# Retention results kept heads by tokens, per-token numbers spread through DRAM, and a new order of work

## What is computed

```
scores = einsum('bhtd,bhsd->bhts', q, k) * mask
denom  = clip(abs(scores).sum(-1, keepdims=True), 1.0, 50000.0)
ret    = einsum('bhts,bhsv->bthv', scores / denom, v)
ret    = ret * rsqrt(mean(ret * ret, axis=-1, keepdims=True) + EPS)
out    = ((x @ W_g + b_g) * ret) @ W_o + b_o
xn     = x / max(norm(x), 1e-12) * sqrt(C) * gamma          # soft mixture
logits = xn @ slots; dispatch = softmax over tokens; combine = softmax over slots
```

## Time and profile before

| | us |
|---|---|
| median of 3 runs (1097.90 to 1098.71) | 1098.13 |
| the profiled execution | 1098.24 |
| its span | 1096.4 |
| PE busy | 1062.8 |
| DVE busy | 960.2 |
| ACT busy | 773.0 |
| POOL busy | 606.9 |

### The profile page before, as it was taken

How to read it: one execution, slowest core, us unless ns; L and a number is a source line. 1 busy time by engine, 2 the same in 40 slices (tenths; PEclk the granted TensorE clock), 3 DMA queues, 4 the chain that set the end, 5 groups by cost and what they waited for, 6 DMA issues and landing times.

```text
span 1096.4 us, 27975 instructions
## 1 busy us (share of the span) xinstructions
PE 1062.8 (97%) x10436; PEld 832.9 (76%) x10436; DVE 960.2 (88%) x2074; ACT 773.0 (71%) x1450; POOL 606.9 (55%) x619
## 2 busy tenths in 40 slices
PE   5799999999999999999999999999999999999997
PEld 3478687787868778687787868778687787868776
DVE  3788989899898988989899898988989899898985
ACT  3476786767777676786767777676786767777674
POOL 2465547556474665547556474655647556474553
PEclk9899999999999999999999999999999999999998
DMA  6000000000000000000000000000000000000000
GB/s 257 11 2 11 1 20 3 1 21 1 21 1 11 11 1 22 1 12 10 2 21 1 21 1 2 20 2 21 2 11 11 2 20 2 21 1 2 11 1 20
DMA packets 18468, 16.97 MB, mean 15 GB/s; under 512 B 800, under 2 KB 17440, under 8 KB 18080
## 3 DMA queue, kind: packets, MB, share of 16 engines
q1 hardware_dynamic: 18336, 15.18, 4.2%
HBM read 10.98 MB, written 4.19 MB: 14 GB/s over the span
## 4 chain that ended last, share of the span: by engine, by line
PE 90%; DVE 6%; issue 1%; ACT 1%; POOL 0%; POOLq 0%; DVEq 0%; ACTq 0%
PE bank L1008 12%; PE bank L959 11%; PE bank L969 10%; PE bank_s L990 7%; PE bank L950 5%; PE bank L979 5%; PE bank L920 5%; PE bank L913 5%; PE bank L1035 3%; DVE ret L661 3%; PE bank L908 3%; PE bank L823 3%; PE bank L874 3%; PE bank L1018 3%; PE bank_s L993 2%; PE bank L854 2%
## 5 line engine op out<-in xcount | busy, mean ns | idle before, releaser
L329 POOL TENSOR_TENSOR ret_abs<-ret_abs 128x512 f32<-128x512 f32 x128 | 168.7, 1318 | 238.2 <-ACT ret_abs L485 238.2
L661 DVE TENSOR_TENSOR ret<-bank_s,k_sb 128x1536 f32<-128x1536 f32 x128 | 223.9, 1749 | 23.7 <-PE bank L1008 14.8
L334 POOL TENSOR_TENSOR urs<-uvar,mhalf 128x16 f32<-128x16 f32 x64 | 185.3, 2903 | 91.8 <-DVE uvar L677 91.8
L485 ACT ACTIVATE ret_abs<-ret 128x1536 f32<-128x1536 f32 x128 | 189.6, 1481 | 8.8 <-DVE ret L661 8.8
L959 PE MATMUL bank<-slotsT,w_sb 128*128 128x128 f32 x1024 | 140.9, 281 | 0.3 <-DVE hact L726 0.3
L969 PEld LDWEIGHTS bank<-w_sb,hact 128*128 128x128 f32 x1024 | 125.5, 192 | 14.7 <-issue 13.9
L969 PE MATMUL bank<-w_sb,hact 128*128 128x128 f32 x1024 | 134.1, 277 | 0.0
L959 PEld LDWEIGHTS bank<-slotsT,w_sb 128*128 128x128 f32 x1024 | 124.3, 192 | 10.3 <-issue 7.4
L340 POOL TENSOR_SCALAR dT<-dT,drec 128x256 f32<-128x256 f32 x128 | 83.4, 665 | 48.6 <-DVE drec L721 48.4
L1008 PE MATMUL bank<-ret,vrow 128*32 128x256 f32 (+1 forms) x2048 | 108.6, 329 | 0.3 <-DVE hact L726 0.2
L990 PE MATMUL bank_s<-qT,km 32*128 32x256 f32 x1024 | 91.4, 426 | 5.0 <-DVE ret L661 5.0
(11 more groups left out here) (143 smaller groups left out, 2397.9 us busy)
## 6 DMA issues: line engine op xcount, KB each, us to landing
x_sb<-x SPq DMA_DIRECT2D x16, 256.0 KB, 2.8
w_sb<-w SPq DMA_DIRECT2D x2, 2048.0 KB, 14.8
out<-attn SPq DMA_DIRECT2D x16, 256.0 KB, 2.3
v_sb<-vectors SPq DMA_DIRECT2D x1, 832.0 KB, 8.1
w_sb<-weights SPq DMA_DIRECT2D x1, 512.0 KB, 5.3
k_sb<-consts SPq DMA_DIRECT2D x1, 466.0 KB, 6.6
w_sb<-weights SPq DMA_DIRECT2D x1, 320.0 KB, 3.2
slot_sb<-slot_rows SPq DMA_DIRECT2D x1, 256.0 KB, 3.5
```

Source lines behind the costliest of these rows:

```text
L329: pool.tensor_tensor(both[:, :, P:SEQ], both[:, :, P:SEQ], both[:, :, SEQ:3 * P], ALU.add)\
L334: pool.tensor_tensor(urs[:, j], uvar[:, j], mhalf[:], ALU.pow).then_inc(ready["urs"].sem, 1)
L485: act.activation(ret_abs[:, q % MR], ret[:, q % MR], ACT.Abs).then_inc(ready["ab"].sem, 1)
L661: dve.tensor_tensor(ret[:, q % MR], bank_s[:, :, 0:3 * P], causal.unsqueeze(1).broadcast_to([P, Q, 3 * P]), ALU.mult)\
```

## The change

- `g`: two quads now share a bank. An odd quad's values sit 16 rows lower in each head's 32 rows (the left operand is read 16 columns earlier), and both accumulate, so that a bank holds eight heads by 256 tokens in columns 0 to 255, and in columns 256 to 511 the denominator, repeated over the 16 rows of each head. Instruction count and columns are those of before.
- `RTc`, `row`, `rowd`, `urs`, `gatedT`, `gTc` are gone. Per two quads: `usq` squares (ACT), `ms` multiplies with a block matrix of 1/16 (PE, one call of 256 columns), `den` clips (DVE), `dsq` squares it with scale sqrt(EPS) (ACT), `ug` multiplies with the gate (DVE), `rx` adds mean and EPS * den^2 (DVE). Per pair: `ln` (ACT) and `rs` (ACT, Exp with scale -0.5) over 128x1024 give the root's inverse, and `gated` multiplies 128x512 twice (DVE). `o` reads that directly.
- `vg` makes only values (2 tasks of two 256-column calls); `gT` makes the gates channels by tokens (2 calls of 512 columns), `gTb` adds the bias (ACT).
- `xn3T`, its copy, `rB` and its copy are gone from PE and ACT. SP writes `rnorm` and `rmax` (128x4 each) to a small DRAM tensor, element by element, and reads each back as 512 numbers to all 128 partitions. `xn3Tc` is now a POOL multiplication of xn2T with what came back; `cs` waits for the other.
- The order of every engine and the banks are new; the last six experts, quad 7, the last two `g`, `out` and `o` are now age 2; stores are age 3 in an order for SP.

```diff
-    "PE": [("qk", 0, 1), ("xn3T", 0, 1), ("qk", 1, 1), ("vg", 0, 1), ...
+    "PE": [("h", 2, 2), ("h", 3, 2), ("quad", 7, 2), ("h", 4, 2), ("ms", 2, 2), ("eo", 2, 2), ("h", 5, 2),
+           ("eo", 3, 2), ("h", 6, 2), ("h", 7, 2), ("eo", 4, 2), ("eo", 5, 2), ("g", 6, 2), ("g", 7, 2),
+           ("xn2T", 0, 1), ("eo", 6, 2), ("eo", 7, 2), ("qk", 0, 1), ("ms", 3, 2), ("qk", 1, 1), ("gT", 0, 1),
+           ("vg", 0, 1), ("out", 0, 2), ("quad", 0, 1), ("xnT", 0, 0), ("out", 1, 2), ("LT", 0, 1),
+           ("quad", 1, 1), ("LT", 1, 1), ("LT", 2, 1), ("o", 0, 2), ("LT", 3, 1), ("s", 0, 0), ("quad", 2, 1),
+           ("g", 0, 1), ("g", 1, 1), ("gT", 1, 1), ("e", 0, 0), ("quad", 3, 1), ("global", 0, 0), ("k", 0, 0),
+           ("ms", 0, 1), ("DT", 0, 1), ("vg", 1, 1), ("DT", 1, 1), ("mxT", 0, 1), ("score", 0, 0), ("r", 0, 0),
+           ("quad", 4, 1), ("g", 2, 1), ("g", 3, 1), ("score", 1, 0), ("DT", 2, 1), ("DT", 3, 1), ("quad", 5, 1),
+           ("PT", 0, 0), ("srow", 0, 0), ("slots", 0, 1), ("PT", 1, 0), ("slots", 1, 1), ("ms", 1, 1),
+           ("o", 1, 2), ("v", 0, 0), ("h", 0, 1), ("local", 0, 0), ("h", 1, 1), ("quad", 6, 1), ("g", 4, 1),
+           ("g", 5, 1), ("eo", 0, 1), ("eo", 1, 1)],
+    "DVE": [("ret", 6, 2), ("prod", 0, 1), ("x1", 0, 1), ("eoc", 0, 2), ("ug", 2, 2), ("hb", 2, 2), ("den", 2, 2),
+            ("hb", 3, 2), ("ret", 7, 2), ("stat2", 0, 1), ("hb", 4, 2), ("rx", 2, 2), ("hb", 5, 2), ("xn2", 0, 1),
+            ("eoc", 1, 2), ("hb", 6, 2), ("cs", 2, 2), ("hb", 7, 2), ("stat", 0, 0), ("eoc", 2, 2), ("ug", 3, 2),
+            ("den", 3, 2), ("cs", 3, 2), ("xn3", 0, 1), ("eoc", 3, 2), ("qkc", 0, 1), ("qkc", 1, 1), ("rx", 3, 2),
...
+            ("gbias", 0, 0), ("drec", 1, 1), ("ret", 3, 1), ("rx", 0, 1), ("vgc", 1, 1), ("rmax", 0, 1),
+            ("LTm", 3, 1), ("drec", 2, 1), ("smax", 0, 0), ("drec", 3, 1), ("ret", 4, 1), ("smax", 1, 0),
+            ("cs", 0, 1), ("ug", 1, 1), ("den", 1, 1), ("zg", 0, 2), ("srowc", 0, 0), ("ka", 0, 0), ("ret", 5, 1),
...
+    "ACT": [("sp", 0, 1), ("usq", 2, 2), ("ab", 6, 2), ("hg", 2, 2), ("hg", 3, 2), ("dsq", 2, 2), ("ab", 7, 2),
+            ("hg", 4, 2), ("hg", 5, 2), ("ce", 1, 2), ("hg", 6, 2), ("hg", 7, 2), ("usq", 3, 2), ("xn2Tc", 0, 1),
+            ("ce", 2, 2), ("dsq", 3, 2), ("ce", 3, 2), ("gTb", 0, 1), ("ln", 0, 2), ("rs", 0, 2), ("ab", 0, 1),
...
+    "SP": [("store", 0, 3), ("load", 0, 0), ("fput", 0, 1), ("fget", 0, 1), ("mput", 0, 1), ("rBc", 0, 1)],
...
+            def mput(p, par, k):
+                sp.wait_ge(*ready["rmax"](p))
+                since(sp, max_got, p - 1)
+                sp.dma_start(turn[1].rearrange("(j p) -> p j", p=P), rmax[:], allow_slow_non_contiguous=True).then_inc(max_put.sem, 16)
+
+            def mget(p, par, k):
+                sp.wait_ge(*max_put(p))
+                since(sp, ready["cs"], p - 1, 3)
+                sp.dma_start(rB[:], turn[1].unsqueeze(0).broadcast_to([P, TOK])).then_inc(max_got.sem, 16)
...
+            def xn3Tc(p, par, k):
+                pool.wait_ge(*got(p))
+                pool.wait_ge(*ready["xn2Tc"](p))
+                since(pool, filled["LT"], p - 1, 3)
+                pool.tensor_tensor(xn3T[:], xn2T[:].rearrange("p b n -> p (b n)"), fB[:], ALU.mult).then_inc(ready["xn3Tc"].sem, 1)
...
+            def ln(p, par, k):
+                act.wait_ge(*ready["rx"](p, DUOS - 1))
+                act.activation(rx[:], rx[:], ACT.Ln).then_inc(ready["ln"].sem, 1)
+
+            def rs(p, par, k):
+
+                act.wait_ge(*ready["ln"](p))
+                act.activation(rx[:], rx[:], ACT.Exp, scale=-0.5).then_inc(ready["rs"].sem, 1)
...
+            def rx_(p, par, h):
+                dve.wait_ge(*filled["ms"](p, h))
+                dve.wait_ge(*ready["dsq"](p, h))
+                dve.wait_ge(*ready["ug"](p, h))
+                since(dve, ready["gated"], p - 1, h // 2)
+                dve.tensor_tensor(rx[:, h], banks[BANK["g", 2 * h]][:, SEQ:], den[:, h % 2], ALU.add).then_inc(ready["rx"].sem, 1)
...
+                bank = banks[BANK["g", q - 1]] if i else claim("g", p, q)
...
+                        at = (Q * (q % Q) + n) * HT - i * VD
+                        left = spread[:, 2 * b + sblock, at:at + HT] if phase < 2 else K["count"][:, (1 - i) * VD:(1 - i) * VD + HT]
                         cols = (0, SEQ) if sblock == 0 else (SEQ, 3 * P)
-                        ins = pe.matmul(bank[n * HT:(n + 1) * HT, sblock * P:SEQ], left,
-                                        src[:, q % MR, n, cols[0]:cols[1]], start=(phase == 0), stop=(phase == 2))
+                        into = (phase // 2 * SEQ + sblock * P, (phase // 2 + 1) * SEQ)
+                        ins = pe.matmul(bank[n * HT:(n + 1) * HT, into[0]:into[1]], left, src[:, q % MR, n, cols[0]:cols[1]],
+                                        start=(i == 0 and phase == 0), stop=(i == 1 and phase == 2))
...
+            def ms(p, par, h):
+                pe.wait_ge(*ready["den"](p, h))
+                pe.wait_ge(*ready["ug"](p, h))
+                pe.matmul(banks[BANK["g", 2 * h]][:, SEQ:], K["heads"], usq[:, h % 2], start=True, stop=True)\
+                  .then_inc(filled["ms"].sem, 1)
```

More of the change, by code:

```diff
@@ L50 @@
 ORDER = {
[10 rows of a table removed]
[L61 to L70, removed]
[3 rows of a table removed]
@@ L103 @@
            "score": "P", "PT": "PTc", "local": ("field", 0), "r": ("tr", 0), "k": ("kr", 0), "v": ("rv", 0),
-           "xn2T": ("xn2Tc", 0), "xn3T": ("xn3Tc", 0), "qk": "qkc", "vg": "vgc", "LT": "LTc", "mxT": ("rmax", 0), "rB": ("rBc", 0), "DT": "Dc", "slots": "slc", "h": "hb", "eo": "eoc", "row": "ug", "g": "RTc", "gatedT": "gTc", "o": "attn",
+           "xn2T": ("xn2Tc", 0), "qk": "qkc", "vg": "vgc", "LT": "LTc", "mxT": ("rmax", 0), "DT": "Dc", "slots": "slc", "h": "hb", "eo": "eoc", "g": "rx", "gT": "gTb", "o": "attn",
@@ L172, in build @@
         km = sb("km", KM, SEQ)
-        vrow, grow = sb("vrow", TILES, HEADS, HT), sb("grow", TILES, HEADS, VD)
+        vrow, grow = sb("vrow", TILES, HEADS, HT), sb("grow", 2, TOK)
         ret, ret_abs = sb("ret", MR, Q, 3 * P), sb("ret_abs", MR, Q, 3 * P)
[L175 to L179, removed]
+        usq, den = sb("usq", 2, SEQ), sb("den", 2, SEQ)
+        ug, rx = sb("ug", DUOS, SEQ), sb("rx", DUOS, SEQ)
         attn = sb("attn", TILES, C)
@@ L214, in build @@
             ("prod", 1), ("x1", 1), ("stat2", 1), ("mv2", 1), ("var_eps2", 1), ("rstd2", 1), ("rn", 3), ("rnorm", 1),
-            ("xn2", 1), ("xn3", 1), ("xn2Tc", 1), ("xn3Tc", 1), ("qkc", 2), ("km", QUADS), ("vgc", 4), ("ret", QUADS),
-            ("ab", QUADS), ("add", QUADS), ("RTc", QUADS), ("usq", 4), ("ug", 4), ("den", 4), ("den2", 4), ("ums", 4),
-            ("uvar", 4), ("urs", 4), ("gated", 4), ("gTc", 2), ("attn", 2), ("LTc", 4), ("mx", 3), ("rmax", 1), ("rBc", 1), ("cs", 4), ("ce", 4),
+            ("xn2", 1), ("xn3", 1), ("xn2Tc", 1), ("xn3Tc", 1), ("qkc", 2), ("km", QUADS), ("vgc", 2), ("gTb", 2), ("ret", QUADS),
+            ("ab", QUADS), ("add", QUADS), ("usq", DUOS), ("den", DUOS), ("dsq", DUOS), ("ug", DUOS),
+            ("rx", DUOS), ("ln", 1), ("rs", 1), ("gated", 2), ("attn", 2), ("LTc", 4), ("mx", 3), ("rmax", 1), ("cs", 4), ("ce", 4),
             ("ltmax", 4), ("DTe", 4), ("drec", 4), ("dn", 4), ("Dc", 4), ("slc", 2), ("hb", E), ("hg", E),
@@ L436, in xn2Tc @@
                     .then_inc(ready["xn2Tc"].sem, 1)
-            def xn3Tc(p, par, k):
-                bank = bank_of("xn3T", p)
-                since(act, filled["LT"], p - 1, 3)
-                act.activation(xn3T[:], bank[:], ACT.Copy).then_inc(ready["xn3Tc"].sem, 1)
             def LTc(p, par, m):
@@ L680, in gated_, with den_ @@
-            def gated_(p, par, j):
-                dve.wait_ge(*ready["urs"](p, j))
-                since(dve, filled["gatedT"], *((p, 0) if j >= 2 else (p - 1, 1)))
-                dve.tensor_tensor(gated[:, j % 2].rearrange("p (h v) -> p h v", h=HEADS), ug[:, j],
-                                  urs[:, j].unsqueeze(2).broadcast_to([P, HEADS, VD]), ALU.mult)\
-                   .then_inc(ready["gated"].sem, 1)
+            def den_(p, par, h):
+                dve.wait_ge(*ready["usq"](p, h))
+                since(dve, ready["rx"], *((p, h - 2) if h >= 2 else (p - 1, h + 2)))
+                dve.tensor_scalar(den[:, h % 2], banks[BANK["g", 2 * h]][:, SEQ:], 1.0, 50000.0, ALU.max, ALU.min)\
+                   .then_inc(ready["den"].sem, 1)
@@ new lines, in ug_ @@
+            def ug_(p, par, h):
+                b, u = divmod(h, 2)
+                dve.wait_ge(*ready["usq"](p, h))
+                dve.wait_ge(*ready["gTb"](p, u))
+                since(dve, filled["o"], p - 1, b)
+                dve.tensor_tensor(ug[:, h], banks[BANK["g", 2 * h]][:, 0:SEQ], grow[:, u, b * SEQ:(b + 1) * SEQ], ALU.mult)\
+                   .then_inc(ready["ug"].sem, 1)
+            def rx_(p, par, h):
[4 more added lines that the diff above has]
```

(11 more changed lines are left out.)

226 lines of the change are left out of this document (102 added, 124 removed), and 30 rows, old and new, of tables (BANK, ORDER).

## The result

The change made the kernel slower: 1249.43 us (median of 4, 1248.27 to 1253.09) against 1098.02 for the kernel before, ratio 1.138 (95% interval 1.136 to 1.141). The forecast of 1073 and its range of 1062 to 1093 were wrong; of the rivals, D happened, the slow write of single numbers, to which I had given 0.04.

The account below looks back on a forecast made before the run. PE was taken to bound the kernel: its period of 65.98 us a pair falls to 64.2, other engines hidden. 16 x 64.2 plus ends of 44 is 1071, plus time over the span gives 1073 us; range 1062 to 1093.

Parts of the forecast that it names:

- D: Rival: SP's write by single numbers is slow; at a 12 us trip, 4 us a pair, 1137 us; chance 0.04.
- the price of the write: SP's write of 512 single numbers to DRAM: 2.8 us, bounds 0 and 14.8; 5.6 for a round trip.
- a cover of 4.4: DVE work before cs 0 (LTm, two drec, two smax, ret) that hides rmax's round trip: 4.4 us.
- half of DVE's room: DVE's standing at cs 0 begins to cost at a trip over some 8 us: 5.6 plus half of 5.9.
- about 11 us: covered: PE work before LT 0, about 11 us, hides rnorm's 1.8, the 5.6 round trip and xn3Tc's 1.3.
- PE's step: On PE, 32 transposes removed (3.5 us) and four ms added (1.75): net -1.75 us a pair, period 64.2.
- ACT 51.4 for 50.3: ACT's work a pair, copies removed, new operations and two table loads added: 48.3 becomes 50.3 us, hidden.
- The tables: ACT's table loads: two more a pair, 2.6 us, bounds none and three; six a pair in all.
- The ends: First and last steps, where PE has too little to do: 3 us more (bounds 0 and some 9), 44 us.
- E: Rival: the new order removes small waits and the ends don't grow: 64.0 and 41, 1067 or less; chance 0.09.
- Rival B: PE waits from the four banks, gT 0 for eoc 3: 0.5 to 1.5 us a pair, 1081 to 1097; chance 0.24.
- C: Rival: Rival B's place but worse, DVE late behind PE's claim of bank 2; at 2.6 us, 1115; chance 0.07.

Follow-up runs that it names:

- Experiment 11: e9_mx_strided plus four extra transfers a pair on SP (single-number writes to neighbours, 64 and 512 bytes apart, and a read back): 1069.05 us.
- e9_mx_strided: e5_rows16 with the transposes before rmax taking every fourth token, so cs reads without a stride: 1070.65 us, 0.975 of the kernel before.
- experiment 3: The changed kernel with both numbers spread by PE and ACT again, nothing through DRAM: 1123.6 us, 1.024 of the kernel before.
- e5_rows16: The changed kernel with each DRAM write as 128 pieces of 16 bytes, cs and xn3Tc reading with a stride: 1088.6 us, 0.991 of the kernel before.
- experiments 7, 8 and 10: Against the kernel before: experiment 3 with rB in bank 1, 1.008; e5_rows16 with cs 0 later, 1.007; e9_mx_strided with xn3 and stat2 moved on DVE, 0.996.

## Why the prediction was wrong

**The step that failed** is the price of the write: "The write has as many pieces as that load's rows, but 4 bytes each: nearest row again 2.8". It took 8.7 us. The count of pieces was taken for what sets a write's time. Experiment 11 shows that it is where they go: 8.9 us against 1.6 to 2.6 with the same count. The read back is a second miss of that step, 4.8 to 4.9 us to landing by the page where the load of x takes 3.0. A trip was 13.7 us, not 5.6. My bound reached to 14.8 for the write alone, so the value was inside it, but it didn't reach the chances: D got 0.04. With 14.8 for the write a trip is 17.6, by D's own price 9.6 us a pair and 1227 us; with a cover of 4.4 the change's sign hung on that term, and the range should have said so.

**D's arithmetic held for half.** It said 4 us a pair at a trip of 12, and from there a microsecond for each microsecond of trip; at 13.7 that is 5.7. Measured against e9_mx_strided, which has the same instructions on PE, the changed kernel's PE stands 159.2 - 29.5 = 129.7 us more, 8.1 a pair: 4.8 more for `srowc`, 2.0 for `xn3T`, which I had called covered, 0.4 for `den` at `ms` (7.1 in all, once, at the end), and 0.8 (13.7 in all) that the profile puts to ACT's `d` or to nothing, nearly all of it in front of the same transposes as `srowc` and in the four pairs in which DVE stands earlier. The other part wasn't in any step: PE's busy time is 1092.0 - 1039.7 = 52.3 us longer, 3.3 a pair, in the same instructions, because work behind the stands runs at clock 0.50. In the groups, the transposes right behind the stand (L887) take 338 ns each against 279. Here every stand of PE over 5 us from the first pair's layer 1 on has this cost. Shorter ones have it sometimes: behind a stand of 1.71 us at 649.81 the granted clock stays at 1.00, and behind one of 1.64 it is 0.50 for 3.4 us.

```profile
798.73 0.70 PE L947 MATMUL bank<-xn3T,snT 128*128 128x256 f32 x2 [1.64 <-POOL xn3T L343]
```
```profile
800.00:803.40 3.40, 3.40 (x21) 2.71 (x18) 1.76 (x1) 1.06 (x3) 1.71 (x3) 0.50 0.02 5
650.00:654.00 4.00, 4.00 (x32) 3.27 (x32) 2.43 (x3) 2.02 (x4) 2.81 (x4) 1.00 0.00 0
```

In experiment 3 it is 3 of 15 stands of 1.9 to 2.1 us. What decides between them these runs don't show. Standing and slower work are together 182 us, which is 1251.2 - 1069.2.

**The cover from "half of DVE's room"** was too kind: at the place shown DVE stood 7.55 and PE 6.62, so 0.9 was absorbed, not the half of 5.9 that D took. DVE's room is a mean over a pair; at one place of the order only what PE has queued ahead of `srowc` counts.

**`rnorm`: "about 11 us: covered".** From the write at 634.47 PE had 13.6 us of work before it stood, the 11 that I counted and two `g` in front of them, and the trip took 14.0 to the start of `xn3Tc`. With the forecast's 5.6 it would have been covered, as e5_rows16 and e9_mx_strided show: there this wait doesn't appear.

**What held.** e9_mx_strided has the change with a trip of 1.4 + 3.8 = 5.2 us for `rmax` and 1.8 + 3.6 = 5.4 for `rnorm` (SP's waits of 22.8 / 16 and 28.7 / 16, and the page's landing times), close to the 5.6 that the sum used, and with it the sum is right: a period of 64.29 for 64.2, 1070.65 us for 1073. PE's step (32 transposes less, four `ms` more, -1.75) is shown by the period, 65.98 to 64.29. DVE has 938.9 / 16 = 58.7 a pair for 58.3, POOL 26.6 for 27.6, ACT 51.4 for 50.3; of ACT's 1.1 only 0.3 is resolved, the two `gTb` at 0.69 in place of 0.62 and the four `dsq` at 0.41 in place of 0.38, and it stays hidden. The tables are six loads a pair as forecast; in the timeline of ACT:

```profile
642.91 1.28 ACT L518 ACT_TABLE_LOAD   x1
644.20 1.06 ACT L518 ACTIVATE rx<-rx 128x1024 f32<-128x1024 f32 x1
645.28 1.28 ACT L523 ACT_TABLE_LOAD   x1
646.57 1.06 ACT L523 ACTIVATE rx<-rx 128x1024 f32<-128x1024 f32 x1
```

`ln` and `rs` take the 1.05 that was interpolated. `rs` loads a table although `ln` is right before it, so the two come from different sets here; the one set for exp and ln of which the Trainium skill tells (page "ScalarE: Activation LUTs", section "Table sets: the hidden batching unit") isn't the one that this kernel gets. And behind each load the next instruction starts at once; of the 1.4 us of drain in that page's section "What ACT_TABLE_LOAD costs" no row here shows anything.

**The ends.** I took 44. e9_mx_strided has 40.6: the ends didn't grow (E's side of that term). The changed kernel's are 49.9, with two trips uncovered.

**Rival B** had the place right and the price low: `gT` waits for `eoc` 3 when DVE is slower by 1.8 us a pair (0.8 us, experiment 5) and doesn't when it isn't (experiment 9). The margin that I put "between 0.9 and nothing" (my own terms give 1.0 without DVE's waits and -0.3 with them) is there, and experiments 7, 8 and 10 show that other places of this order have one as thin. **C** didn't occur. **D's page**, the Trainium skill's "DMA: Bandwidth & Descriptors", section "Rules for kernel authors", had the sign: it tells one not to write with a non-contiguous last dimension. The runs agree, with 8.7 us against 1.2 to 2.0. One descriptor per element, of which that section speaks, isn't enough to explain the price: as many elements take 1.6 us when they are 512 bytes apart.

## What to carry to other kernels

A transfer whose form no row of the profile shows, put on a path with less cover than its upper bound, isn't a term with a nearest value: the sign of the change hangs on it, and its chance is to be given accordingly. When numbers go through DRAM, lay them so that each partition writes one run, and put the rearrangement where it is free (here in the column step of a transpose, 11 ns each) and not on an engine that has no room. And price a stand of PE twice: for itself, and for the work behind it at half clock, which here followed every stand over 5 us and some of 1.6 us and more.

## What the runs showed of the hardware that I had not expected

- 512 writes of 4 bytes to neighbouring addresses of DRAM take 8.9 us on SP's wait, with 64 bytes between them 2.6, with 512 bytes 1.6; as 128 writes of 16 neighbouring bytes 1.2 to 2.0.
- A read of the same 2 KB to each of 128 partitions lands after 4.8 to 5.0 us behind a write of single numbers, after 3.3 to 4.2 behind one of 16-byte pieces, and a load of x of the same size after 2.8 to 3.0.
- A tensor_tensor of 128x512 in float32 on DVE takes 1134 ns with one of its operands read at a stride of 16 bytes, 689 to 690 without.
- Behind a stand of PE of 6.6 us the granted clock was 0.50 over the next 3.3 us of work; behind one of 1.7 us it was 1.00, behind one of 1.6 us 0.50.
